# Five chunks in flight on TensorE, one for each stage, with double-buffered masked maxima, in a graph layer with segment maxima

## The reference

```python
h = relu(layernorm(x))                               # 12500 x 32
e_feat = concatenate([h[src], h[dst], edge_attr])    # 412500 x 96
v = relu(e_feat @ W1 + b1) @ W2 + b2                 # 96 -> 64 -> 32
x_cand = segment_max(v, dst, num_segments=12500)
return x + maximum(x_cand, h)
```

## Time and profile before

| | |
|---|---|
| median of 3 runs | 5345.29 us (5330.25 to 5361.33) |
| the profiled execution | 5326.15 us, its span 5324.3 us |
| mean granted TensorE clock | 0.829 |
| PE busy | 3680.6 us (69%), 19060 matmuls |
| PE weight loads | 2578.9 us (48%) |
| POOL busy | 2701.2 us (51%), 2824 gathers |
| DVE busy | 2212.2 us (42%) |
| ACT busy | 982.3 us (18%) |

### The profile page before, as it was taken

The page is one execution under the profiler, slowest core; times in us unless marked ns, Lnnn a source line. Parts: engine busy times, 40 slices in busy tenths (PEclk is TensorE's granted clock), DMA queues, the critical chain, the costliest instruction groups (busy, mean ns, idle before and its releaser), DMA issues.

```text
span 5324.3 us, 74917 instructions
## 1 busy us (share of the span) xinstructions
PE 3680.6 (69%) x19060; PEld 2578.9 (48%) x19060; DVE 2212.2 (42%) x6394; ACT 982.3 (18%) x2055; POOL 2701.2 (51%) x2853
## 2 busy tenths in 40 slices
PE   1577676667766777767776667676766767667777
PEld 1355454444544454545555445454544544445545
DVE  4344334344433444434444334343443443334436
ACT  2111111111111111111111111111111111111111
POOL 5455555554545455555555454555555555545551
PEclk9788888788888888888888888887887888878889
DMA  4222222222222222222222212222222222212222
GB/s 112 56 45 43 41 43 41 41 41 44 44 41 41 42 45 43 43 41 46 44 43 44 41 38 44 41 45 40 43 42 40 43 45 43 41 40 46 43 42 39
DMA packets 612176, 237.39 MB, mean 45 GB/s; under 512 B 328651, under 2 KB 609632, under 8 KB 612158
## 3 DMA queue, kind: packets, MB, share of 16 engines
q1 hardware_dynamic: 411534, 137.78, 10.7%
q0 software_dynamic: 91008, 46.57, 9.0%
q10 hardware_dynamic: 109616, 52.85, 3.4%
HBM read 227.75 MB, written 9.11 MB: 44 GB/s over the span
## 4 chain that ended last, share of the span: by engine, by line
another core or an unknown queue 43%; PE 29%; issue 14%; DVE 6%; ACT 5%; DVEq 1%; ACTq 1%; DMA 1%; SPq 0%
PE ps_spare L593 9%; PE ps_hid L547 5%; PE ps_hid L537 5%; PE ps_hid L543 3%; DVE hot L931 2%; PE ps_val L556 2%; PE ps_picked L578 2%; ACT hidden L726 2%; PE ps_turned L567 2%; PE ps_feat L528 2%; ACT feat_t L736 1%; ACT ps_biased L747 1%; DVE best L980 1%; ACTq L683 1%
## 5 line engine op out<-in xcount | busy, mean ns | idle before, releaser
L473 POOL DMA_INDIRECT feat<-h_rows,idx_ring x2824 | 2690.0, 953 | 2528.5 <-DMA idx_ring<-src_in 1661.4
L593 PE MATMUL ps_spare<-hot,table 128*128 128x256 f32 x10028 | 1920.8, 331 | 223.8 <-issue 221.0
L593 PEld LDWEIGHTS ps_spare<-hot,table 128*128 128x128 f32 x10028 | 1508.2, 212 | 574.4 <-issue 539.7
L980 DVE TENSOR_TENSOR best<-ps_picked,best 32x64 f32 x1612 | 354.8, 220 | 1495.6 <-remote 1358.8
L537 PE MATMUL ps_hid<-feat_t,w_blk 128*128 128x512 f32 x806 | 554.3, 777 | 515.9 <-ACT feat_t L736 387.0
L931 DVE TENSOR_SCALAR hot<-key_ring,class_at 128x256 fp32r<-128x256 f16 x2613 | 787.4, 369 | 98.3 <-remote 67.3
L726 ACT ACTIVATE hidden<-ps_hid,b_col 128x512 f32<-128x512 f32 x403 | 277.3, 688 | 1954.3 <-remote 1081.2
L567 PE MATMUL ps_turned<-ident,running 128*128 128x128 f32 x806 | 180.7, 310 | 567.9 <-DVE running L945 345.4
L547 PE MATMUL ps_hid<-edge_hot,term_ring 128*128 128x512 f32 x806 | 555.1, 776 | 0.7 <-DVE edge_hot L953 0.7
L967 DVE TENSOR_TENSOR ends<-ps_turned,ends 128x256 fp32r<-128x256 f32 x403 | 170.4, 423 | 731.7 <-ACT ends L731 416.3
L938 DVE SCALAR_TENSOR_TENSOR masked<-key_ring,group_at,ps_spare 128x256 f32<-128x256 f16 x400 | 174.0, 477 | 652.5 <-remote 584.3
(11 more groups left out here) (112 smaller groups left out, 1467.5 us busy)
## 6 DMA issues: line engine op xcount, KB each, us to landing
attr_ring<-edge_attr_in ACTq DMA_DIRECT2D x403, 128.0 KB
loc_ring<-loc_rows SPq DMA_DIRECT2D x403, 128.0 KB
feat<-h_rows,idx_ring POOLq DMA_INDIRECT x2824
keep_ring<-keep_rows SPq DMA_DIRECT2D x403, 64.0 KB
key_ring<-key_rows SPq DMA_DIRECT2D x201, 128.0 KB
term_ring<-term_rows SPq DMA_DIRECT2D x806, 16.0 KB
idx_ring<-src_in SPq DMA_DIRECT2D x403, 4.0 KB
end_ring<-end_rows SPq DMA_DIRECT2D x403, 2.0 KB
```

The source lines that it names most:

```text
L473: nc.gpsimd.indirect_dma_start(feat[:, slot, k, 0:D], None, h_dram, bass.IndirectOffsetOnAxis(ap=idx_ring[:, slot, k:k + 1].bitcast(U32), ...
L593: mm = pe.matmul(row_sums[t], table[half][:, at:at + Q, :].rearrange("p t d -> p (t d)"), hot[:, c, :], start=(c == 0 and t == 0 and half ...
L980: mm = nc.vector.tensor_tensor(col, ps_pick[D * q:D * q + D, WIN * q:WIN * q + WIN], col, ALU.max)
```

## The change

PE's step becomes turn_features(v), first_layer(v-1), second_layer(v-2), turn_ends(v-3), pick_ends(v-4): five chunks in flight, each stage one step after the one that feeds it. ACT's and DVE's steps follow. `masked` gets two buffers, so that the sums of a batch are masked before the first layer has used those of the batch before, and a batch is dealt out over the last part of an odd step and the first part of an even one. The auxiliary inputs are loaded for chunk s-4 in SP's step s (LAG), as their slot now comes free two steps later. 11 steps are written out ahead of the loops instead of 3 (PRE); the 3 chunks that gather all 8 columns have a constant of their own (FULL). `best` is cleared in two halves, ahead of the steps. At the end one more batch is selected in whole.

The diff, without the drains behind the loops, the places where PRE only becomes FULL, and the order of two drains:

```diff
-PRE = 3
-LAG = 2
+FULL = 3
+PRE = 11
+LAG = 4
...
-        masked = sb("masked", [P, 2, 2 * MIX])
+        masked = sb("masked", [P, 2, 2, 2 * MIX])
...
             def next_key(i, n):
-                sp.wait_ge(S["mask_done"], i * 8 + 2 * (n - KEYS + 2))
-                load_key(i * 8 + (PRE + 2 * n), n % KEYS)
+                sp.wait_ge(S["mask_done"], i * 8 + 2 * (n - KEYS + 1))
+                load_key(i * 8 + (FULL + 2 * n), n % KEYS)
...
             next_key(0, BATCHES)
+            next_key(0, BATCHES + 1)
...
-                if not known(i) or v >= PRE:
-
-                    m, part = i * 4 + (v - PRE) // 2, (v - PRE) % 2
-                    pe.wait_ge(S["mask_done"], m * 2 + 4)
+                if v >= FULL:
+                    m, part = i * 4 + (v - FULL) // 2, (v - FULL) % 2
+                    pe.wait_ge(S["mask_done"], m * 2 + 2)
                     for t in range(2):
-                        pe.matmul(ps_hid[HID:P, 2 * P:3 * P], w1_rep[:], masked[:, t, MIX * part:MIX * part + MIX],
+                        pe.matmul(ps_hid[HID:P, 2 * P:3 * P], w1_rep[:], masked[:, (v - FULL) // 2 % 2, t, MIX * part:MIX * part + MIX],
...
-                    if c == 0:
-                        pe.wait_ge(S["mask_done"], m * 2 + 2)
+                    if c == 0 and not (known(m) and m == 0):
+                        pe.wait_ge(S["mask_done"], m * 2)
...
-            GAPS = (((0, 1), (2,), (3, 4), (5,), (6,)), ((7, 8), (9, 10), (11, 12), (), ()))
+            GAPS = (((6, 7), (8, 9), (10, 11), (12,), ()), ((), (), (0, 1), (2, 3), (4, 5)))
 
             def step(i, v):
-                if not known(i) or v == PRE - 1:
-                    gaps = GAPS[(v - PRE + 1) % 2]
-                    m = i * 4 + (v - PRE + 1) // 2
-                else:
-                    gaps = ((),) * 5
-                    m = 0
-                if later(i, v):
+                m = i * 4 + (v - 1) // 2
+                gaps = GAPS[v % 2] if v else ((),) * 5
+                turn_features(i, v)
+                select(m, gaps[0])
+                if v >= 1:
                     first_layer(i, v - 1)
-                select(m, gaps[0])
-                if later(i, v - 1):
-                    turn_ends(i, v - 2)
                 select(m, gaps[1])
-                turn_features(i, v)
+                if v >= 2:
+                    second_layer(i, v - 2)
                 select(m, gaps[2])
-                if later(i, v):
-                    second_layer(i, v - 1)
+                if v >= 3:
+                    turn_ends(i, v - 3)
                 select(m, gaps[3])
-                if later(i, v - 1):
-                    pick_ends(i, v - 2)
+                if v >= 4:
+                    pick_ends(i, v - 4)
                 select(m, gaps[4])
...
             def step(i, v, at):
+                take_features(i, v, at)
                 if later(i, v):
                     rectify(i, v - 1)
                 if later(i, v - 1):
-                    take_ends(i, v - 2)
-                take_features(i, v, at)
-                if later(i, v):
-                    add_bias(i, v - 1)
+                    add_bias(i, v - 2)
+                if later(i, v - 2):
+                    take_ends(i, v - 3)
...
+            dve.wait_ge(S["loc_staged"], NB)
+            nc.vector.memset(best[:, T * HID:NP_ROWS], 0.0).then_inc(S["best_zero"], 1)
+
             node_terms(dve, nc.vector.tensor_copy, 1)
...
-            EARLY, LATE = range(0, 7), range(7, CLASSES)
+            EARLY, LATE = range(0, 6), range(6, CLASSES)
 
             def step(i, v):
-                if later(i, v - 1):
+
+                place_edges(i, v)
+                if v % 2 == 0:
+                    build_hot(i, v // 2, EARLY)
+                else:
+                    build_hot(i, v // 2, LATE)
+                if v >= 2:
                     scan(i, v - 2)
-                place_edges(i, v)
-                if not known(i):
-                    if (v - PRE) % 2 == 0:
-                        build_hot(i, (v - PRE) // 2 + 1, EARLY)
-                        split_ends(i, v - 2)
-                        mask_rows(i, (v - PRE) // 2)
-                    else:
-                        build_hot(i, (v - PRE) // 2 + 1, LATE)
-                        split_ends(i, v - 2)
-                elif v:
-                    build_hot(i, 0, (EARLY, LATE)[v - 1])
-                    if v > 1:
-                        split_ends(i, v - 2)
-                if later(i, v):
-                    place_ends(i, v - 1)
-                if later(i, v - 1):
-                    keep_best(i, v - 2)
-                if known(i):
+                if v >= 2 and v % 2 == 0:
+                    mask_rows(i, v // 2 - 1)
+                if v >= 3:
+                    split_ends(i, v - 3)
+                    place_ends(i, v - 3)
+                if v >= 4:
+                    keep_best(i, v - 4)
+                if known(i) and v < FULL:
                     dve.wait_ge(S["feat_turned"], v + 1)
                     nc.vector.memset(feat[:, v, Q - 1, 0:D], 0.0).then_inc(S["cols_cleared"], 1)
-                if known(i) and v == 1:
-                    dve.wait_ge(S["term_stored"], 16 * (1 + len(h_parts)))
-                    nc.vector.memset(best[:], 0.0).then_inc(S["best_zero"], 1)
...
+            dve.wait_ge(S["term_stored"], 16 * (1 + len(h_parts)))
+            nc.vector.memset(best[:, 0:T * HID], 0.0).then_inc(S["best_zero"], 1)
+            steps(dve, step, {0: check})
```

More of the change, by code:

```diff
@@ L56, in gnn_layer @@
     NP_ROWS = T * P + WIN
-    BATCHES = (C - PRE) // 2
+    BATCHES = (C - FULL) // 2
     CLASSES = -(-T // GROUP)
@@ L60, in gnn_layer @@
     assert ONE_TILE
-    assert D == 32 and HID == 64 and W2.shape[1] == D and (C - PRE) % RING == 0
+    assert D == 32 and HID == 64 and W2.shape[1] == D and (C - PRE) % RING == 0 and (C - FULL) % 2 == 0
     FULLP = N // T
@@ L71, in gnn_layer @@
     end_dram = nc.dram_tensor("end_rows", (C, CE), BF16, kind="Internal").ap()
-    key_dram = nc.dram_tensor("key_rows", (PRE + 2 * BATCHES + 2, 2 * MIX), F16, kind="Internal").ap()
+    key_dram = nc.dram_tensor("key_rows", (FULL + 2 * BATCHES + 4, 2 * MIX), F16, kind="Internal").ap()
     def rows_of(b):
@@ L152, in gnn_layer @@
         key_part = [z.bitcast(I32).rearrange("p (b e) -> p b e", b=NB)
-                    for z in (any_dst_h[:].rearrange("p b c -> p (b c)"), masked[:].rearrange("p t e -> p (t e)"))]
+                    for z in (any_dst_h[:].rearrange("p b c -> p (b c)"), masked[:, 0, :, :].rearrange("p t e -> p (t e)"))]
         key_stage = key_ring[:].rearrange("p k c a e -> p (k c a e)")[:, 0:NB * 2 * MIX].rearrange(
@@ L240, in got @@
             per = 16 * (COLS - 1)
-            return 16 * COLS + turn * per if slot < PRE else turn * per + per
+            return 16 * COLS + turn * per if slot < FULL else turn * per + per
         def any_steps(eng, any_step):
@@ L367, in _ @@
             sp.wait_ge(S["zeros_ready"], 1)
-            sp.dma_start(key_dram[C:C + 2, :].rearrange("c (p k) -> (c p) k", k=32), zeros[0:16, 0:16].bitcast(F16)
+            sp.dma_start(key_dram[C:C + 4, :].rearrange("c (p k) -> (c p) k", k=32), zeros[0:32, 0:16].bitcast(F16)
                          ).then_inc(S["key_stored"], 16)
@@ L378, in _ @@
             for m in range(KEYS):
-                load_key(PRE + 2 * m, m)
+                load_key(FULL + 2 * m, m)
             sp.wait_ge(S["firsts_in"], 32)
@@ L471, in step @@
                 for k in range(COLS):
-                    if k != Q - 1 or (known(i) and v < PRE):
+                    if k != Q - 1 or (known(i) and v < FULL):
                         nc.gpsimd.indirect_dma_start(
@@ L635, in clear_mixed @@
                 pe.wait_ge(S["cols_cleared"], RING)
-            steps(pe, step, {1: begin_mixed, PRE - 1: clear_mixed})
+            steps(pe, step, {0: begin_mixed, RING - 1: clear_mixed})
             first_layer(0, C - 1)
+            second_layer(0, C - 2)
+            turn_ends(0, C - 3)
+            pick_ends(0, C - 4)
+            second_layer(0, C - 1)
             turn_ends(0, C - 2)
-            second_layer(0, C - 1)
+            pick_ends(0, C - 3)
+            turn_ends(0, C - 1)
             pick_ends(0, C - 2)
-            turn_ends(0, C - 1)
             pick_ends(0, C - 1)
@@ L775, in _ @@
             rectify(0, C - 1)
+            add_bias(0, C - 2)
+            take_ends(0, C - 3)
+            add_bias(0, C - 1)
             take_ends(0, C - 2)
-            add_bias(0, C - 1)
             take_ends(0, C - 1)
@@ L837, in _ @@
             nc.vector.memset(h_win[:, T - 1:Q * TG, :], 0.0).then_inc(S["pads"], 1)
-            for slot in range(PRE, RING):
+            for slot in range(FULL, RING):
                 nc.vector.memset(feat[:, slot, Q - 1, 0:D], 0.0).then_inc(S["cols_cleared"], 1)
@@ L905, in _ @@
             nc.vector.tensor_copy(key_stage[:, :, 1, :], high).then_inc(S["key_staged"], 1)
-            for t in range(2):
```

(18 more changed lines are left out.)

2 lines of the change are left out of this document (1 added, 1 removed).

## The result

The kernel after the change took 5449.66 us (median of 4 runs, 5447.75 to 5460.15) against 5337.77 us of the kernel before beside it: a ratio of 1.0295, 95% interval [1.0178, 1.0411]. It is slower, by 1.8 to 4.1%, where 9% faster was forecast. Its profiled execution took 5460.15 us, its span is 5458.3 us.

A forecast was written before the change was run, and what follows sets the result against it. The prediction took POOL's pauses, waiting for PE signals that its own gathers hold up, to bound the kernel. Sum: 5326.15 - 467 (pauses) - 5 (clearing `best`) + 6 (drain) = 4860 us; range 4430 to 5450.

The forecast's parts named there:

- What bounds the kernel: Whole kernel: while POOL gathers, PE's signals come late or not at all, bunched 1.8 to 2.9 us after the last gather.
- Depth: PE's step: each stage's inputs are signalled one step earlier, so POOL gathers two chunks, 14 columns, in one burst.
- Size: POOL's pauses: 5.91 us for two chunks, 2.96 us a chunk in place of 4.12, saving 467 us.
- upper bound of 8.71: POOL's pause for two chunks, at most the longest normal one shown: 4.36 us a chunk, a loss of 97 us.
- rival 2: SP's queue: index load behind pick_ready and load_aux makes pauses 8.9 us, +133 us, 5460 us; chance 0.20.
- it fits: PE's work for two steps, 18.1 us, fits in POOL's two-chunk burst with its tail, 19.3 us.
- The drain: End of the kernel: two more steps to drain while POOL is silent, +6 us, between 0 and 24.
- Clearing `best` in halves: Start of the kernel: the larger-address half moves to an earlier time when DVE waits for PE, 5 us less.
- The last batch: End of the kernel: one whole batch instead of its first half, 22 matmuls under other work, costing nothing.
- The masks: Masked maxima in two buffers, mask_rows moved: no instruction more per chunk, hidden by PE's work, costed at nothing.
- Rival 3: No change: the array itself is behind during gathers, or each pause frees one chunk; 5326 us, give or take 25; chance 0.10.

The follow-up runs named there:

- a_onegather: The kernel after the change with one gather for a chunk instead of 7, so the output is another: 3119.46 us.
- a_poolbusy: The kernel after the change with one gather for a chunk and six iotas with drains in place of the six others: 3420.39 us.
- after_2: The kernel after the change, unchanged, run once more: 3629.45 us against 3639.64 of the kernel before, 0.9969.
- a_idx: a_lag6 with indices loaded once chunk s-8 is gathered, POOL itself waiting for feat_turned: 4730.02 us, 0.8885 of the kernel before; run again, 3643.53 us.
- b_idx: b_lag4 with indices loaded early and POOL itself waiting for feat_turned, as in a_idx: 3640.73, 3637.97, 3635.37 and 3634.28 us in four runs.
- a_lag6: The kernel after the change, auxiliary inputs loaded for chunk s-6 instead of s-4: 5128.18 us, 0.9615 of the kernel before; repeats 3644.83 and 3643.22 us.
- the gap kernels: a_idx with iotas and drains behind each chunk's gathers: 5006.41 us with two iotas, 4586.27 and 4557.32 us with one.
- b_lag4: The kernel before the change with auxiliary inputs loaded for chunk s-4 instead of s-2: 5336.51 us, 1.0034 of the kernel before.

## Why the prediction was wrong, point by point

**What bounds the kernel: right where it was read.** A chunk is 8.74 us of gathering and a pause, and POOL waits for the signals that its gathers hold. a_onegather and a_poolbusy show it to be the gathers' DMAs. But I took the hold for a property of the hardware. It was there in the first runs (the kernel before at 5330 to 5350 us), and not in after_2, a_idx_2, b_idx, a_lag6's repeats and the gap kernels (the kernel before at 3640 us): the same program.

**Depth: right as to the order of the work, wrong as to what a pair is worth.** The waits at L567 for the scan (345.4 us in the earlier trace rows) are gone from the list of waits, turn_features goes out 2.5 us behind the bunch (2538.39, where 1.5 was forecast), and nearly all bursts are pairs. But pairs weren't new: 281 pauses for 403 chunks meant that the kernel before had 116 of them already. a_lag6 against b_lag4 (0.9615 against 1.0034) shows that the depth is worth 4%, and only with SP out of the way. Even then it isn't by pairs: a_lag6 has 118 bursts of two chunks, as many as the kernel before, and shorter pauses behind them.

**Size: the step that failed.** It is the sentence "I take today's mean pause, 5.91 us, since SP sometimes comes late". That mean mixes two kinds. In the trace of the kernel before, the pauses behind a burst of one chunk are 3.8 us long on average (158 of them) and those behind a burst of two 8.55 us (116). The sum needed the second number for its pairs and took the mean of both; with 8.55/2 = 4.28 us a chunk in place of 4.12 it would have forecast a small loss. The change then measured 9.02 us a pause, beyond even the upper bound of 8.71 that I had taken from one pause of three chunks in flight. Its SP part had been written down as rival 2: pick_ready stands at the end of PE's step, and the index load queues behind load_aux. With 9.02/2 = 4.51 us a chunk the sum gives 5326 + 157 + 1 = 5484, and 5460 was measured. What I used against rival 2, the pause of 5.81 after a burst of 14, was among the seven shortest of those 116.

**What the sum did not have.** With 18.1 us of PE work for a pair and 19.3 us of burst I wrote "it fits". It doesn't always, since PE itself slows down late in a long burst, to one matmul in some 2 us. The first trace had it too, in 19 of its 278 bursts against 134 of 200 after the change (counted where PE twice in a row stands over 0.9 us between matmuls of one line):

```profile
1522.14 0.37 PE L593 MATMUL ps_spare<-hot,table 128*128 128x256 f32 x1 [1.84 <-issue]
...
1525.02 0.37 PE L593 MATMUL ps_spare<-hot,table 128*128 128x256 f32 x1 [2.51 <-issue]
...
1528.07 0.37 PE L593 MATMUL ps_spare<-hot,table 128*128 128x256 f32 x1 [2.68 <-issue]
```

I take it for the reason why a_lag6 stopped at 5128 and a_idx at 4730. That is not shown: the gap kernels, which were to test it, ran only where nothing is held.

**Small terms.** The drain was sized right: from the last transposes of features to the last maxima 13.4 us before (5282.8 to 5296.2), 19.9 after (5410.1 to 5430.0), +6.5 for my +6. Clearing `best` in halves saved more than 5 us: chunk 1's first layer had started at 164.0, and starts at 154.2 now. It is not what made after_2 10 us faster than 3640: a_lag6_2 and a_idx_2 clear `best` in the same way and take 3645 and 3644 us, and the traces differ in the gathers, 947 ns each in after_2 and 953 and 954 in those two, for a reason that stays open. The last batch costs nothing that shows, as forecast. The masks were put at nothing, "hidden by PE's work in between", and are not hidden: before its first class of a batch `select` waits for the mask of the batch before, which DVE now makes behind the scan. This wait isn't in the trace of the kernel before, and it is 265.2 us of PE's time after the change. What it adds to the time, no run shows.

**The rivals.** Rival 2 happened, with chance 0.20. Rival 3 (the array itself is behind) is half true in a way that I had excluded: late in a burst PE is behind, and its starts show it, though earlier ones are on time. What a burst slows isn't PE alone: SP's next load after loc_ring's, with no semaphore between them in the code, comes 0.8 us later as a rule, and over 2 us later for 65 of 403 chunks before, 96 after, and none in after_2. The Trainium skill's rule that the signal is pushed when PSUM has acknowledged (Perfetto Trace Analysis, section Tensor Engine Instruction) leaves room for both the late signals and the slowed matmuls; no run here shows where in that path they are held.

**What to have looked at.** The pauses by the length of the burst before them, for which the trace had all rows. The chances gave 0.72 to faster because I trusted the mechanism of depth. But its gain had to pass through SP's queue, and the change itself moved the event that SP waits for (pick_ready, which came two steps behind a chunk's turn_features and now comes four behind) while LAG kept the distance exactly as tight as it had been.

## What to carry to other kernels

When a pipeline is made deeper, list every in-order queue that waits for a stage's last event and give each the slack that the engines got; here two steps of it on SP turned +3% into -4%. Work that one queue issues behind an unrelated wait (indices behind auxiliary loads) belongs ahead of that wait, or on a wait of its own, which brought another 8%. When a change is to turn many short events into fewer long ones, take the cost of a long one from those that the trace already has, not from the mean of both kinds. And run the kernel before again, at other times and on other chips, before trusting a mechanism: a stall that is most of the profile in one run can be absent from the next, and with it the whole question.

## What was not expected of the hardware

- While indirect DMAs of 128 rows are issued back to back, PE's signals to ACT, DVE and SP came late in the runs with the kernel before at 5330 us, by 14 us in the rows shown (ACT at 2580.47 for transposes that ended by 2566.70), the last of them in a bunch, 1.8 to 2.9 us after the last gather in the pauses shown; ACT reacted within 0.1 us when POOL was silent. In after_2 and the other traces from runs with the kernel before at 3640 us there was none of it. What differs between them is not shown.
- In such a burst, after 12 us in the one shown and never before 7 in these traces, PE goes on with one instruction in 1.4 to 3 us, signals or not (L595 and L593 above; 8 of them take 1.2 us otherwise).
- With this gone PE's mean granted clock is 0.96 to 1.00 instead of 0.80 to 0.87 (0.88 to 0.91 in the gap kernels, where PE waits more). The idle stretches, and not the matmuls, had it at its lower level of 1.2 GHz: behind the work that ended at 2569.4 the kernel before was granted 1.00 until 2572, 0.73 from there to 2574, and 0.50 from 2574 to 2586, with PE at work again since 2581.
- The same one-hot comparison on DVE takes 670 ns beside POOL's iotas in a_poolbusy and 355 ns in a_onegather. It is not what sets a_poolbusy's time, since POOL waits for no engine there:

```profile
L943 DVE TENSOR_SCALAR hot<-key_ring,class_at 128x256 fp32r<-128x256 f16 x797 | 480.5, 670 | 0.0
```

```profile
L937 DVE TENSOR_SCALAR hot<-key_ring,class_at 128x256 fp32r<-128x256 f16 x884 | 250.2, 355 | 0.0
```
